# Two of eight clips of a pair moved to ScalarE as Relu passes, one sum tile per pair, ones products of 256 columns

## What is computed

```python
q = (lat @ Wq).reshape(b, n, HEADS, DHEAD).transpose(0, 2, 1, 3)
k = apply_rope(k, cos[None, None], sin[None, None])
scale = DHEAD ** (-0.5)
attn = jnp.einsum('bhnd,bhsd->bhns', q, k) * scale
attn = jnp.clip(attn, -11.0, 11.0)
attn = jax.nn.softmax(attn, axis=-1)
out = jnp.einsum('bhns,bhsd->bhnd', attn, v)
...
out = jnp.einsum('bseh,ehv,bse->bsv', scores, values, sel)   # experts, second phase
```

## Time and profile before

| | |
|---|---|
| median of 3 runs | 1026.55 us (1025.08 to 1026.93) |
| profiled execution | 1027.25 us, its span 1025.5 us |
| TensorE busy | 975.7 us (95% of the span) |
| VectorE busy | 828.9 us (81%) |
| ScalarE busy | 516.8 us (50%) |
| GpSimd busy | 255.9 us (25%) |

### The profile page before, as it was taken

How to read it: one execution, slowest core, us unless ns; L and a number is a source line. 1 busy time by engine, 2 the same in 40 slices (tenths; PEclk the granted TensorE clock), 3 DMA queues, 4 the chain that set the end, 5 groups by cost and what they waited for, 6 DMA issues and landing times. The chain is left out here.

```text
span 1025.5 us, 15252 instructions
## 1 busy us (share of the span) xinstructions
PE 975.7 (95%) x5336; PEld 612.3 (60%) x5336; DVE 828.9 (81%) x1226; ACT 516.8 (50%) x735; POOL 255.9 (25%) x228
## 2 busy tenths in 40 slices
PE   3889999999999999999999999999999889999998
PEld 2645555555665555555555555555655368888886
DVE  7689999999998999999989887999889876545422
ACT  4645555556555656565555555555555442222221
POOL 3433423121211121221312100320000145445443
PEclk9989999999999999999999999999999999999999
DMA  5533333332323233232323223222222471232321
GB/s 157 188 123 100 103 88 109 99 93 68 94 68 94 73 99 89 73 89 79 111 78 93 77 84 83 84 83 83 84 63 64 147 253 57 111 130 111 111 82 42
DMA packets 68952, 100.34 MB, mean 98 GB/s; under 512 B 21968, under 2 KB 44752, under 8 KB 66832
## 3 DMA queue, kind: packets, MB, share of 16 engines
q1 hardware_dynamic: 68880, 99.41, 31.8%
HBM read 70.01 MB, written 10.75 MB: 79 GB/s over the span
## 5 line engine op out<-in xcount | busy, mean ns | idle before, releaser
L1105 ACT ACTIVATE wide_a<-score_ps 128x1024 f32<-128x1024 f32 x256 | 249.1, 1027 | 117.3 <-PE score_ps L904 117.2
L1368 DVE TENSOR_SCALAR wide_a<-wide_a 128x1024 f32<-128x1024 f32 x256 | 186.9, 759 | 44.8 <-ACT wide_a L1105 44.7
L1377 DVE TENSOR_TENSOR p_sum<-wide_a 128x1024 f32<-128x1024 f32 x128 | 159.4, 1245 | 2.3
L917 PE MATMUL o_ps<-wide_a,values_a 128*64 128x512 f32 x512 | 124.9, 608 | 2.6 <-issue 2.3
L917 PE MATMUL o_ps<-wide_a,v_sb 128*64 128x512 f32 x512 | 124.9, 607 | 2.4 <-DVE wide_a L1368 1.0
L1911 DVE SCALAR_TENSOR_TENSOR act<-h_ps,wide_a 128x512 f32<-128x512 f32 x64 | 44.2, 691 | 90.0 <-PE h_ps L149 82.2
L904 PE MATMUL score_ps<-q_hi,k_hi 64*128 64x512 f32 x512 | 114.9, 445 | 0.9 <-DVE k_lo L1347 0.9
L904 PEld LDWEIGHTS score_ps<-q_hi,k_hi 64*128 64x128 f32 x512 | 48.0, 184 | 110.5 <-issue 78.3
L1682 POOL TENSOR_TENSOR act_lo<-act,act_hi 128x512 fp32r<-128x512 f32 x64 | 84.8, 1325 | 96.5 <-ACT act_hi L1828 96.5
L1828 ACT CAST act_hi<-act 128x512 fp32r<-128x512 f32 x64 | 39.7, 621 | 135.7 <-DVE act L1911 135.7
L904 PE MATMUL score_ps<-q_hi,k_lo 64*128 64x512 f32 x512 | 101.6, 393 | 0.0
(11 more groups left out here) (232 smaller groups left out, 2005.8 us busy)
## 6 DMA issues: line engine op xcount, KB each, us to landing
wide_a<-sel_dram SPq DMA_DIRECT2D x16, 1024.0 KB, 4.8
k_swap<-k SPq DMA_DIRECT2D x124, 128.0 KB, 2.3
w_hi<-packs_hi SPq DMA_DIRECT2D x26, 384.0 KB, 2.9
w_lo<-packs_lo SPq DMA_DIRECT2D x26, 384.0 KB, 3.6
den<-inv_dram SPq DMA_DIRECT2D x64, 128.0 KB, 2.8
ctx_raw<-ctx SPq DMA_DIRECT2D x24, 128.0 KB, 2.3
packs_hi<-w_hi SPq DMA_DIRECT2D x8, 384.0 KB, 3.2
packs_lo<-w_lo SPq DMA_DIRECT2D x8, 384.0 KB, 3.7
```

The source lines that it names most:

```text
L917: mm = pe.matmul(o_ps[DH * h:DH * h + DH, :], v_sb[n // 2 % 2][:, at:at + DH], probs[s % RING][:, h, :], start=(s == 0), stop=(s == STEPS ...
L1105: act.activation(probs[s % RING][:], score_ps[s % 2][:], ACT.Exp, scale=DH ** -0.5).then_inc(exp_done, 1)
L1368: dve.tensor_scalar(probs[s % RING][:], probs[s % RING][:], CLIP_HI, CLIP_LO, ALU.min, ALU.max).then_inc(clipped, 1)
L1377: dve.tensor_tensor(p_sum[m][:], first, second, ALU.add).then_inc(summed_up, 1)
```

## The change

Tiles 1 and 7 of each pair (`ACT_CLIPS`) are clipped before the exponential, on ScalarE, in three passes: Relu(score/8 + 11) from PSUM into the probs buffer, Relu(22 - that) in place, and Exp(11 - that) in place. The bounds stand in a small SBUF tile `lift` (11 and 22), which is the bias operand. `exp_done` is given by the first pass, `act_clipped` by the last. VectorE no longer clips these tiles; `sum_up` and TensorE's `attend` wait for `act_clipped` where they need them. A third level of sums, `sum_all`, adds the two `sum_quad` tiles into `p_sum[3]`, in the next pair's m = 0, between `sum_quad` and `add_y`. The four ones products read that one tile, 256 columns each, and the halves of the columns land in the groups of 32 rows. So `evac_o` copies 256 columns, `den_rows` has one value instead of two, and the small addition L177 goes.

```diff
@@ -40,6 +40,8 @@
 LATE_X = 11
+LIMIT = 11.0
+ACT_CLIPS = (1, 7)
 DUO = 2 * P
@@ -166,17 +167,15 @@
             at = DH * h + QUAD * e
-            row = sh.den[at:at + 1, :].rearrange("a (p j) -> a p j", p=DH)
-            sp.dma_start(sh.den_rows[DH * h:DH * h + DH, e, :], row).then_inc(sh.den_turned, DMA)
+            row = sh.den[at:at + 1, 0:NQ // 2].rearrange("a (p j) -> a p j", p=QUAD)
+            sp.dma_start(sh.den_rows[at:at + QUAD, :], row).then_inc(sh.den_turned, DMA)
...
     wait(dve, sh.inv_stored, DMA * n)
-    dve.tensor_tensor(sh.inv_rows[:], sh.den_rows[:, 0, :], sh.den_rows[:, 1, :], ALU.add).then_inc(sh.den_added, 1)
-    wait(dve, sh.den_added, n + 1)
-    dve.reciprocal(sh.inv_rows[:], sh.inv_rows[:]).then_inc(sh.den_inv, 1)
+    dve.reciprocal(sh.inv_rows[:], sh.den_rows[:]).then_inc(sh.den_inv, 1)
@@ -478,6 +482,14 @@
             return job_ps[1 - f % 2][:]
+        def act_clips(n, s):
+            return len(ACT_CLIPS) * n + sum(c <= s for c in ACT_CLIPS)
+        def dve_clips(n, s):
+            return STEPS * n + s + 1 - act_clips(n, s)
@@ -757,6 +769,8 @@
             pool.memset(power[:], -0.5).then_inc(power_ready, 1)
+            for i in range(2):
+                pool.memset(lift[:, i:i + 1], LIMIT * (i + 1)).then_inc(lift_ready, 1)
             pool.wait_ge(power_ready, 3)
@@ -911,7 +925,10 @@
                     wait(pe, o_evac, n)
-                pe.wait_ge(clipped, g + 1)
+                if s in ACT_CLIPS:
+                    pe.wait_ge(act_clipped, act_clips(n, s))
+                else:
+                    pe.wait_ge(clipped, dve_clips(n, s))
                 for h in range(2):
@@ -920,15 +937,15 @@
-                pe.wait_ge(quads_up, 2 * n + 2)
+                pe.wait_ge(all_up, n + 1)
                 pe.wait_ge(ones_ready, 1)
...
                         at = DH * h + QUAD * e
-                        mm = pe.matmul(side_ps[at:at + QUAD, :], ones[:], p_sum[2 * e + 1][:, h, :],
-                                       start=True, stop=True)
+                        mm = pe.matmul(side_ps[at:at + QUAD, 0:NQ // 2], ones[:],
+                                       p_sum[3][:, h, e * (NQ // 2):(e + 1) * (NQ // 2)], start=True, stop=True)
                 mm.then_inc(den_ready, 1)
@@ -1102,7 +1119,17 @@
                 wait(act, summed_up, MACROS * n + (s - RING) // 2 + 1)
-                act.activation(probs[s % RING][:], score_ps[s % 2][:], ACT.Exp, scale=DH ** -0.5).then_inc(exp_done, 1)
+                p_ = probs[s % RING][:]
+                if s not in ACT_CLIPS:
+                    act.activation(p_, score_ps[s % 2][:], ACT.Exp, scale=DH ** -0.5).then_inc(exp_done, 1)
+                    return
+                act.activation(p_, score_ps[s % 2][:], ACT.Relu, bias=lift[:, 0:1], scale=DH ** -0.5).then_inc(exp_done, 1)
+                act.wait_ge(exp_done, g + 1)
+                act.activation(p_, p_, ACT.Relu, bias=lift[:, 1:2], scale=-1.0).then_inc(lifted, 1)
+                act.wait_ge(lifted, act_clips(n, s))
+                act.activation(p_, p_, ACT.Exp, bias=lift[:, 0:1], scale=-1.0).then_inc(act_clipped, 1)
@@ -1113,7 +1140,7 @@
                 wait(act, o_scaled, n)
-                act.copy(den[:], side_ps[:]).then_inc(den_evac, 1)
+                act.copy(den[:, 0:NQ // 2], side_ps[:, 0:NQ // 2]).then_inc(den_evac, 1)
@@ -1364,14 +1392,17 @@
                 g = STEPS * n + s
+                if s in ACT_CLIPS:
+                    return
                 dve.wait_ge(exp_done, g + 1)
...
-                dve.wait_ge(clipped, STEPS * n + 2 * m + 2)
-                if m % 2 == 1:
+                dve.wait_ge(clipped, dve_clips(n, 2 * m + 1))
+                wait(dve, act_clipped, act_clips(n, 2 * m + 1))
+                if m == 3:
                     wait(dve, den_ready, n)
@@ -1381,6 +1412,11 @@
                 dve.tensor_tensor(second[:], first[:], second[:], ALU.add).then_inc(quads_up, 1)
+            def sum_all(n):
+                dve.wait_ge(quads_up, 2 * n + 2)
+                dve.tensor_tensor(p_sum[3][:], p_sum[1][:], p_sum[3][:], ALU.add).then_inc(all_up, 1)
@@ -1467,6 +1503,7 @@
                         sum_quad(n - 1, 1)
+                        sum_all(n - 1)
                     if m == 0 and n >= 3:
@@ -1508,6 +1545,7 @@
             sum_quad(NPAIR - 1, 1)
+            sum_all(NPAIR - 1)
             split_o(dve, sh, NPAIR - 2, 0)
```

More of the change, by code:

```diff
@@ L101, in shared_state @@
     sh.den = sb("den", [P, NQ])
-    sh.den_rows = sb("den_rows", [P, 2, NQ // DH])
+    sh.den_rows = sb("den_rows", [P, NQ // DH])
     sh.inv_rows = sb("inv_rows", [P, NQ // DH])
@@ L123, in shared_state @@
     sh.den_turned = sem("den_turned")
-    sh.den_added = sem("den_added")
     sh.den_inv = sem("den_inv")
@@ L298, in attention_phase @@
         power = sb("power", [P, 4])
+        lift = sb("lift", [P, 2])
         carry_pool = sb("carry_pool", [P, 2])
@@ L392, in attention_phase @@
         exp_done = sem("exp_done")
+        lift_ready = sem("lift_ready")
+        lifted = sem("lifted")
+        act_clipped = sem("act_clipped")
         clipped = sem("clipped")
@@ L395, in attention_phase @@
         quads_up = sem("quads_up")
+        all_up = sem("all_up")
         pv_done = sem("pv_done")
@@ L1128, in _ @@
             act.wait_ge(power_ready, 3)
+            act.wait_ge(lift_ready, 2)
             act.activation(carry_act[:], power[:, 0:1], ACT.Exp)
```

## The result

| | median of runs (us) | ratio to before, 95% interval |
|---|---|---|
| before | 1026.73 (1025.08 to 1028.42, 6 runs) | |
| after | 1053.99 (1051.96 to 1057.75, 6 runs) | 1.0271 [1.0248, 1.0295] |

The change costs 27.3 us; the forecast of 1052 was 25.5 above the median before. The runs of the kernel after spread over 5.8 us; the profiled one is its slowest, 1057.75 us with a span of 1056.0, 30.5 more than the span before.

A forecast was written before the change was run, and what follows sets the result against it. TensorE was taken as the bound, two ScalarE-VectorE chains less than 0.4 us behind. Stage losses of 15.5, 4.4, 4.8 and 0.5 us made 25.2, added to 1026.55 for a forecast of 1052; range 1034 to 1067.

The forecast's parts named there:

- Bound now: Whole kernel: TensorE bounds it, with two chains through ScalarE and VectorE less than 0.4 us behind.
- TensorE's saving: Ones products on TensorE: half the columns save 0.45 us per pair, 14 us over 32 pairs.
- The trio, K's copies: ScalarE: three passes take 3.46 us against 1.03; K's second copy ends 10.15 us after tile 6's exponential starts, 1.72 later.
- The K chain: K's copies, swap DMA, rotation, q_lo, V product: decides the period, 1.12 us more per pair.
- my own condition: TensorE's waits: the K chain is wrong if TensorE's idle time stands before o_ps products instead of the V product.
- 5.43 us: Time from K's second copy through the swap DMA to the rotation on VectorE, read in the pair of 610 us.
- The o chain: Exponentials, VectorE's list to o_lo, copy of o_ps, product: 12.87 us against 12.21, 0.66 more, so not deciding.
- The sum of the stages: All stages together: 25.2 us more, from 15.5, 4.4, 4.8 for the first six pairs and 0.5 for the last two.
- Middle: 16 pairs at 24.16 us today: 25.13 each, 15.5 us more in all.
- Next eight: Eight pairs at 24.45 us today: 25.0 each, 4.4 us more in all.
- TensorE sets the pace: Rival: ScalarE's idle 41% takes the passes, TensorE gains 14 us, giving 1012.5; 9%.
- only the o chain binds: Rival: the swap's time shrinks when it starts later, about 0.4 us x 26 pairs, 1037; 14%.

The follow-up runs named there:

- kernel 1: Kernel before plus only the third-level sum and the 256-column ones products, all eight clips on VectorE: 1051.25 us (1.0228).
- 3: Kernel after with o_lo moved ahead of the sum of tiles 0 and 1 and the statistics on VectorE: 1058.95 us (1.0297).
- kernel 9: Kernel 1 with sum_all left out: 256-column products only, half of the softmax's sum missing: 1014.32 us (0.9884).
- kernel 10: Kernel after with sum_all left out, both three-pass clips on ScalarE, half of the softmax's sum missing: 1037.28 us (1.0120).
- 5: Kernel after with o_lo moved earlier and tile 1's second and third pass put behind K's copies on ScalarE: 1054.72 us (1.0275).
- kernel 12: Kernel after with sum_all behind o_lo and the ones products behind attend 1: 1053.17 us (1.0263).
- 2: Kernel before with only the clips of tiles 1 and 7 moved to ScalarE, sums and 512-column products unchanged: 1041.91 us (1.0142).

## Why the prediction came out, and where it did not

- *Bound now.* Half right. Attend 0 and the V product had no slack, and kernels 1 and 3 show each of them wait. But what stood right behind the V product was VectorE's own list, not the swap of K (see below). I took VectorE's 92.5% as a reason why a wait cannot be made up; it is the period itself, together with the way through ScalarE, 1.9 us. Had I added up VectorE's loop, the sum alone would have been priced at about 0.8 us per pair.
- *TensorE's saving.* 0.45 forecast, 0.42 measured; worth 12 us if nothing else changes (kernel 9).
- *The trio, K's copies.* 3.46 and 10.15 us forecast, 3.48 and 10.16 measured.
- *The K chain decides.* Wrong in the middle stretch. By my own condition, TensorE's idle time stands before the o_ps products. The failing term is the 5.43 us from K's copy to the rotation, taken from one pair. The trace of the kernel before could have told. Its four swap DMAs in the pair of 432 us, where K's copy ends at 440.78, and those of the pair of the earlier trace rows:

```profile
L560 SPq DMA_DIRECT2D k_swap<-k x4: 554/590/592, 440.8 to 442.7; - x4
...
DMA to landing us min/median/max: 2.3/2.3/2.3
```

```profile
L560 SPq DMA_DIRECT2D k_swap<-k x4: 554/594/599, 609.7 to 611.6; - x4
...
DMA to landing us min/median/max: 2.3/2.3/3.4
```

  The last of the first four was issued at 442.7 and landed 2.3 us later, at 445.0: 4.2 us after the copy and 1.5 before the rotation at 446.52, not 0.3. So it was in 14 of the 16 middle pairs; in the pair that I read, one DMA took 3.4. With 4.3 in place of 5.43 my own sum puts the V product at 19.29 us after tile 6's exponential, where it was, and the K chain costs nothing. In kernel 10, where the rotation waits for the swap, it was 4.32 us in one pair (375.83 to 380.15) and 5.82 in the next but one (424.45 to 430.27). ScalarE's timeline of kernel 10:

```profile
374.76 1.07 ACT L1095 COPY k<-job_ps 128x512 f32<-128x512 f32 x2
...
423.39 1.06 ACT L1095 COPY k<-job_ps 128x512 f32<-128x512 f32 x2
```

and the rotations on VectorE behind these copies:

```profile
380.15 1.23 DVE L1365 TENSOR_TENSOR k<-k,cos_sb 128x1024 f32<-128x1024 f32 x1 [0.47 <-DMA k_swap<-k]
...
430.27 1.23 DVE L1365 TENSOR_TENSOR k<-k,cos_sb 128x1024 f32<-128x1024 f32 x1 [1.95 <-DMA k_swap<-k]
```

  With 4.3 the rotation could start at 14.5 after tile 6's exponential; VectorE reaches it at 14.82 by its own list. In the kernel after no rotation of the middle 16 pairs waits for the swap; six of the later ones do. In three of them (602.87 to 682.81 us), where one of the four DMAs took 3.8 or 3.9 us, the K chain binds as forecast.
- *The o chain.* Its size was near: attend 0 forecast 12.87 us after tile 6's exponential, measured 13.07 (458.41 - 445.34). Of the 0.2 missing, 0.11 is the new sum, which waits for the quad sum and so does not overlap it (1.25, not 1.14), and 0.09 the wait behind the trio. I had it as a rival with 14% and priced it at 0.4 us per pair; in the middle 16 it is where TensorE waits, at 0.52 per pair. It is one stretch of VectorE's loop, though, and kernels 3 and 5 show that with the trios in place nothing is gained by relieving it.
- *The sum of the stages.* The total of 25.2 against 27.3 (30.5 in the profiled run) is two errors that cancel, so that it came this near is luck. Middle: 15.5 forecast, 8.3 measured. Next eight: 4.4 forecast, 13.3 measured. There the sum alone costs 1.4 (197.0 against 195.6) and the trios with small products 2.5 (198.1), and only both together 13.3 (5.0 with the sum behind o_lo, kernel 12). 6.9 of it are the three pairs in which the K chain binds, with a spell at the lower clock in the second; in the fourth the casts of keys push the trio, VectorE's extra rows and the sum push add_y, the ones products wait, o_lo is slow, and the clock falls again. Which of these costs how much was not tried. The first six: 4.8 forecast, 7.3 measured.
- *The rivals.* "TensorE sets the pace" is refuted by 1 and 2; "only the o chain binds", because the swap's 5.43 us shrinks, was right on where TensorE waits in the middle stretch and 17 us short, since it left the late stretch at nothing. I did not have as a rival what the experiments point to, the loop of VectorE and ScalarE.

## What to carry to other kernels

Follow each engine's list once round: if an engine has no wait but one, and that one comes back to itself through another engine, its work plus that bridge is a period of its own, even when its busy share is below TensorE's, and each instruction added to its work costs its full length. Work taken off a nearly full engine bought nothing here, since it returned as three dependent passes that the engine must wait for in order. Take the latency of a DMA from its landings in several pairs, not from the one in which an engine was seen to wait for it: that one is the slow one.

## What the runs showed of the hardware

- A pass over 1024 columns on ScalarE with a bias column took 1.11 us from PSUM and 1.15 from SBUF; a step that waits for the one before starts 0.03 to 0.04 us after its end. The Trainium skill (ScalarE: Activation LUTs, section "What ACT_TABLE_LOAD costs") gives about 280 ns plus 0.833 ns per column, 1.13 us for 1024: the trace agrees within 0.02 us, and has the SBUF pass above it.
- The four swap DMAs were issued within 1.9 us and each landed 2.3 us after its issue in most pairs, the last one 4.2 to 4.3 us after K's copy; in other pairs of the same kernels one or more of them took longer, up to 5.5 us, and the rotation started up to 7.5 us after the copy (640.85 in the kernel before). What sets this was not found.
- The granted clock fell to 0.50 for the eight products at 687.35, which took 3.49 us instead of 1.94, after TensorE had been idle for 2.32 us, and it fell once more in that stretch (0.63 from 639 to 642 us) after an idle time of 1.78. In kernel 1, after 2.31 us of idle time before the same products (682.30), it stayed at 1.00 and they took 1.94. So the idle time just before doesn't settle it; where the clock fell, the wait at 687 cost 1.5 us more than itself.
- o_lo on VectorE lasted 2.86 us instead of 0.68 at 683.72. GpSimd's subtraction of 1024 columns ran from 683.13 to 686.03 beside it:

```profile
683.13 2.90 POOL L766 TENSOR_TENSOR wide_lo<-w_raw,wide_hi 128x1024 fp32r<-128x1024 f32 x1
```

  o_lo ended 0.55 us after it. In kernel 1 the same two meet (o_lo at 678.68 for 2.86, the subtraction from 678.08 to 680.98), and in the kernel before the subtraction (662.83 to 665.20) meets a clip of VectorE, which lasts 1.78 us instead of 0.69 and ends 0.55 after it too. That the one holds up the other is what the three have in common; it was not tried.
